# Attention on TensorE: 128-column products between 512-column ones, probabilities one unit later, the value product in one bank

## What is computed

```python
ada = (timestep_embed @ ada_w + ada_b)[:, None, :]
shift1, scale1, gate1, shift2, scale2, gate2 = jnp.split(ada, 6, axis=-1)
x1 = _ln(x) * (1.0 + scale1) + shift1
qkv = (x1 @ qkv_w + qkv_b).reshape(Bc, Tc, 3, H, DH)
q, k, v = (qkv[:, :, 0], qkv[:, :, 1], qkv[:, :, 2])
attn = jnp.einsum('bthd,bshd->bhts', q, k) * scale
attn = jax.nn.softmax(attn, axis=-1)
attn_out = jnp.einsum('bhts,bshd->bthd', attn, v).reshape(Bc, Tc, INNER)
attn_out = attn_out @ out_w + out_b
x = x + gate1 * attn_out
x2 = _ln(x) * (1.0 + scale2) + shift2
h = jax.nn.gelu(x2 @ ffn_w1 + ffn_b1, approximate=False)
x = x + gate2 * (h @ ffn_w2 + ffn_b2)
...
h = jnp.square(jax.nn.relu(jnp.einsum('bsd,hd->bsh', x, w1)))
return jnp.einsum('bsh,dh->bsd', _rms_norm(h), w2)   # w1, w2 ternary
```

## Time and profile before

| | |
|---|---|
| median of 3 runs | 390.71 us (390.7 to 392.43) |
| span of the profiled execution | 391.2 us |
| PE busy | 367.8 us (94%), 2096 matmuls |
| DVE busy | 288.0 us (74%) |
| ACT busy | 237.0 us (61%) |
| POOL busy | 129.7 us (33%) |
| mean granted clock of PE | 0.980 of full speed |

### The profile page before, as it was taken

The page is one execution under the profiler, slowest core; times in us unless marked ns, Lnnn a source line. Parts: engine busy times, 40 slices in busy tenths (PEclk is TensorE's granted clock), DMA queues, the critical chain, the costliest instruction groups (busy, mean ns, idle before and its releaser), DMA issues. The chain is left out here.

```text
span 391.2 us, 6260 instructions
## 1 busy us (share of the span) xinstructions
PE 367.8 (94%) x2096; PEld 319.5 (82%) x2096; DVE 288.0 (74%) x486; ACT 237.0 (61%) x582; POOL 129.7 (33%) x111
## 2 busy tenths in 40 slices
PE   2899999999999999999999999999889899996975
PEld 2789888888888888888888898889778787885855
DVE  5775569768776976866887667689988638797793
ACT  1464576665666566656676566775687358573751
POOL 1522224321542232272323144335423300162451
PEclk9999999999999999999999999999999999998995
DMA  7913031000303100030200012010000000000002
GB/s 231 358 61 108 1 109 54 2 0 3 108 0 107 54 0 0 0 107 29 78 0 0 0 26 83 0 55 1 2 0 1 2 0 2 0 1 2 8 19 80
DMA packets 11778, 16.53 MB, mean 42 GB/s; under 512 B 672, under 2 KB 7920, under 8 KB 11760
## 3 DMA queue, kind: packets, MB, share of 16 engines
q1 hardware_dynamic: 11760, 16.30, 12.6%
HBM read 15.25 MB, written 1.05 MB: 42 GB/s over the span
## 5 line engine op out<-in xcount | busy, mean ns | idle before, releaser
L345 POOL TENSOR_TENSOR prob<-prob,rinv 128x512 f32<-128x512 f32 x32 | 33.4, 1043 | 152.4 <-DVE rinv L788 152.4
L980 PE MATMUL bank<-x_hi,wqk_hi 128*128 128x512 f32 x128 | 54.4, 425 | 0.0
L982 PE MATMUL bank<-x_hi,wqk_lo 128*128 128x512 f32 x128 | 51.3, 401 | 0.0
L981 PE MATMUL bank<-x_lo,wqk_hi 128*128 128x512 f32 x128 | 51.1, 399 | 0.0
L706 DVE TENSOR_TENSOR v_lo<-bank,v_hi 128x512 fp32r<-128x512 f32 x30 | 20.7, 691 | 39.2 <-ACT v_hi L427 39.2
L493 ACT ACTIVATE prob<-bank,nbias 128x128 f32<-128x128 f32 x128 | 45.1, 370 | 4.1 <-DVE nbias L782 4.1
L427 ACT ACTIVATE p_split<-bank 128x512 fp32r<-128x512 f32 x32 | 19.1, 598 | 35.4 <-PE bank L1014 35.4
L461 ACT ACTIVATE o_hi<-pv_pair,bias 128x512 fp32r<-128x512 f32 x31 | 21.3, 688 | 24.3 <-PE pv_pair L1029 24.3
L982 PE MATMUL bank<-k_hi,q_lo 128*128 128x128 f32 x128 | 35.4, 276 | 0.0
L417 POOL TENSOR_TENSOR raw_qk<-raw_qk 128x512 f32<-128x512 f32 x13 | 18.4, 1415 | 50.7 <-ACT raw_qk L622 50.4
L981 PE MATMUL bank<-k_lo,q_hi 128*128 128x128 f32 x128 | 35.2, 275 | 0.0
(11 more groups left out here) (206 smaller groups left out, 1086.9 us busy)
## 6 DMA issues: line engine op xcount, KB each, us to landing
raw_qk<-in_L_cond_qkv_w_dram SPq DMA_DIRECT2D x8, 512.0 KB, 4.9
raw_v<-in_L_cond_qkv_w_dram SPq DMA_DIRECT2D x4, 512.0 KB, 3.8
raw_o<-in_L_cond_out_w_dram SPq DMA_DIRECT2D x4, 512.0 KB, 3.6
xt<-in_x_dram SPq DMA_DIRECT2D x2, 512.0 KB, 5.0
xr<-in_L_cond_ada_w_dram SPq DMA_DIRECT2D x1, 1024.0 KB, 10.2
raw_w<-in_L_cond_ffn_w_dram SPq DMA_DIRECT2D x2, 512.0 KB, 7.6
t_raw<-in_L_ffn_W_fc_dram SPq DMA_DIRECT2D x4, 256.0 KB, 3.8
t_raw<-in_L_ffn_W_proj_dram SPq DMA_DIRECT2D x4, 256.0 KB, 3.9
```

The lines of the kernel that those rows point to most:

```text
L345: nc.gpsimd.tensor_tensor(e, e, rinv[:, j % 2, :].unsqueeze(2).broadcast_to([P, SQ, P]), ALU.mult).then_inc(norm_done, 1)
L980: nc.tensor.matmul(dst, ah, bh, start=start and n == 0, stop=False)
L981: nc.tensor.matmul(dst, ah, bl, start=False, stop=False)
L982: m = nc.tensor.matmul(dst, al, bh, start=False, stop=stop and n == len(terms) - 1)
```

## The change

- On PE a unit starts with the 12 matmuls of q and k of unit i+1. Behind each of the first four stands one transpose, now of the probabilities of unit i-2, and behind the other eight one score matmul of unit i. A v block follows, one in each of the units 2 to 29, with the last four score matmuls and the first three of the value product; then the out product of unit i-3 with the other nine.
- The probabilities of unit i are transposed in unit i+2 and no longer in i+1, their value product is taken there as well, and the out product in i+3.
- The scores have two banks in turn (3 and 5), q and k two buffers in turn; the second buffers are parts of w2_hi and w2_lo, so half of the second FFN weight is cast after attention.
- The value product is 12 matmuls of 128 columns into bank 4, three a sequence, and its output one pass on DVE.
- Behind the loop, unit 30 has an order of its own ("early") and unit 31 is written out.
- ACT, DVE and POOL programs follow, with weight casts moved by one or two units; on POOL normalise stands behind them.

Bank table, ACT's and DVE's units:

```diff
-BQ, BK, BV, BS, BO, BY = 0, 1, 2, 3, 4, 6
+BQ, BK, BV, BO, BY = 0, 1, 2, 4, 6
+BS = (3, 5)
...
+        heads_q = ((q_hi[:, :], q_lo[:, :]), (w2_hi[:, w2_fourth], w2_lo[:, w2_fourth]))
+        heads_k = ((k_hi[:, :], k_lo[:, :]), (w2_hi[:, w2_third], w2_lo[:, w2_third]))
         w1_chunks, wv_chunks, wo_chunks = (
...
-        pv_main, pv_rest = (pv_pair[:, :].rearrange("p (s x t) -> p s x t", s=SQ, x=2)[:, :, n, :] for n in range(2))
+
+        bank = [ctx.enter_context(nc.psum_tensor(f"bank{n}", [P, TQ], F32)) for n in range(8)]
 
 
         cond_in, arow_in, bias_in, ada1_in, ada2_in = (
...
 
-        V_AT = {1: (4, 5), 2: (6, 7), 5: (0, 1), 6: (2, 3)}
...
+            def unit(G, j, last=False):
+                i = UG * G + j
+                known = isinstance(i, int)
+                early = known and i == NU - 2
+                if early:
+                    o_hi_part(*earlier(G, j, 3))
+                if not known or i >= 2:
+                    p_hi_part(i - 2)
+                q_hi_part(*later(G, j))
+                if not early and (not known or i >= 3):
+                    o_hi_part(*earlier(G, j, 3))
+                k_hi_part(*later(G, j))
+                load_weights(G, j, last)
+                if has_v(i):
+                    v_hi_part(V_AT[j], v_count(i))
+                if j == 5 and not last:
+                    for k in range(KD):
+                        wv_hi_part(k, 16 * G + 32)
+                softmax_exp(i, j)
 
...
+            def o_lo_part(G, j):
+                hi, lo = head_output(UG * G + j)
+                biased_lo(lo, bank[BO], HG * G + VB + j % HG, hi, o_h, UG * G + j + 1, o_l)
+
...
+            def unit(G, j):
                 i = UG * G + j
...
-                    dve.wait_ge(xr_done, 1)
-                    stats_of(2, xr)
-                if last and j == UG - 1:
-                    normalise(2, xr)
+                known = isinstance(i, int)
+                early = known and i == NU - 2
+                if early:
+                    o_lo_part(*earlier(G, j, 3))
+                if not known or i >= 1:
+                    softmax_inverse(i - 1, (j - 1) % 2)
+                if not known or i >= 2:
+                    p_lo_part(i - 2)
+                q_lo_part(*later(G, j))
+                if not early and (not known or i >= 3):
+                    o_lo_part(*earlier(G, j, 3))
+                if early:
+                    accumulate(i - 3, G, 0, last=True)
+                    softmax_max(i, j)
+                    gate(0)
+                    k_lo_part(*later(G, j))
```

The matmuls' steps, PE's unit, and PE's and DVE's programs behind unit 30:

```diff
+            def score_step(j, n):
+
+                (qh, ql), (kh, kl), t = heads_q[j % 2], heads_k[j % 2], slice(n // 3 * P, (n // 3 + 1) * P)
+                m = three(bank[BS[j % 2]][:, t], n % 3, qh[:, t], ql[:, t], kh[:, t], kl[:, t], True, True)
+                if n == 11:
+                    m.then_inc(s_mm, 1)
...
+            def pv_step(j, n):
+
+                a, quad, s = j % HG, j // HG, n // 3
+                b, h, t = quad * SQ + s, slice(a * P, (a + 1) * P), slice(s * P, (s + 1) * P)
+                m = three(bank[BO][:, t], n % 3, v_hi[:, b, h], v_lo[:, b, h], p_split[:, s, 0, :], p_split[:, s, 1, :], True, True)
+                if n == 11:
+                    m.then_inc(pv_mm, 1)
...
-                    b, h = quad * SQ + s, slice(a * P, (a + 1) * P)
-                    at = 2 * s * P
-
-                    nc.tensor.matmul(pv_pair[:, at:at + 2 * P], v_hi[:, b, h], p_split[:, s, :, :].rearrange("p x t -> p (x t)"),
-                                     start=True, stop=False)
-                    m = nc.tensor.matmul(pv_pair[:, at:at + P], v_lo[:, b, h], p_split[:, s, 0, :], start=False, stop=True)
-                m.then_inc(pv_mm, 1)
...
+            def unit(G, j):
...
-                    transpose_x(2, bank[0:2])
+                (G1, j1), (G2, j2), (G3, j3) = later(G, j), earlier(G, j, 2), earlier(G, j, 3)
+                VG = G + 1 if j in (6, 7) else G
+                early = known and i == NU - 2
+                pe.wait_ge(wqk_l, HG * G1 + j1 % HG + 1)
+                pe.wait_ge(q_l, i + 1)
+                t = not known or i >= 2
+                if t:
+                    transpose_ready(i - 2, v_count(i - 1) if not known or i - 1 <= V_LAST else v_count(V_LAST))
+                for n in range(6):
+                    q_or_k_step(G1, j1, 0, n)
+                    if t and n < 4:
+                        transpose_step(j2, n)
+                    else:
+                        if n == (4 if t else 0):
+                            scores_ready(G, j)
+                        score_step(j, n - 4 if t else n)
+                if early:
+                    out_ready(G3, j3)
+                    for n in range(6):
+                        out_step(G3, j3, n)
+                        score_step(j, n + 2)
+                for n in range(6):
+                    q_or_k_step(G1, j1, 1, n)
+                    if not t:
+                        score_step(j, n + 6)
+                    elif early and n < 4:
+                        score_step(j, n + 8)
+                    elif not early:
+                        score_step(j, n + 2)
...
+                if early:
+                    pv(G2, j2)
+                    return
+                pe.wait_ge(wv_l, KD * VG + KD)
+                pe.wait_ge(p_l, i - 1)
+                for n in range(6):
+                    v_step(VG, V_AT[j], n)
+                    if n < 4:
+                        score_step(j, n + 8)
+                    else:
+                        if n == 4:
+                            pv_ready(G2, j2)
+                            pv_step(j2, 0)
+                            pv_step(j2, 1)
+                        else:
+                            pv_step(j2, 2)
+                if known and i == 2:
+                    for n in range(3, 12):
+                        pv_step(j2, n)
+                    return
+                out_ready(G3, j3)
+                for n in range(6):
+                    out_step(G3, j3, n)
+                    if n % 2 == 0:
+                        pv_step(j2, 3 + n // 2 * 3)
+                        pv_step(j2, 4 + n // 2 * 3)
+                    else:
+                        pv_step(j2, 5 + n // 2 * 3)
...
+            for j in range(3, UG - 1):
+                unit(NG - 1, j)
+            L = NG - 1
+            transpose_p(NU - 3)
+            scores_ready(L, UG - 1)
+            for n in range(12):
+                score_step(UG - 1, n)
+            pe.wait_ge(gated, 1)
+            out_ready(L, UG - 4)
+            for n in range(6):
+                out_step(L, UG - 4, n)
+                if n < SQ:
+                    transpose_y_step(0, n)
+            pv(L, UG - 3)
+            transpose_p(NU - 2)
+            transpose_xr(0, bank[0:2])
+            out_product(L, UG - 3)
+            pv(L, UG - 2)
+            transpose_p(NU - 1)
+            out_product(L, UG - 2)
+            pe.wait_ge(xrT_done, 1)
+            transpose_x(2, bank[0:2])
+            pv(L, UG - 1)
...
+
+            softmax_inverse(NU - 2, (NU - 2) % 2)
+            p_lo_part(NU - 3)
+            o_lo_part(NG - 1, UG - 4)
+            softmax_max(NU - 1, UG - 1)
+            add_residual(0)
+            dve.wait_ge(xr_done, 1)
+            stats_of(2, xr)
+            o_lo_part(NG - 1, UG - 3)
+            p_lo_part(NU - 2)
+            softmax_inverse(NU - 1, (NU - 1) % 2)
+            normalise(2, xr)
             o_lo_part(NG - 1, UG - 2)
-            modulate(2, SHIFT2, SCALE2, bank[0:2], lambda: p_lo_part(NU - 1))
-            o_lo_part(NG - 1, UG - 1, h2[:, 0, :])
+            p_lo_part(NU - 1)
+            modulate(2, SHIFT2, SCALE2, bank[0:2])
+            o_lo_part(NG - 1, UG - 1)
             ternary_compare(NG - 1, -1)
```

453 lines of the change are left out of this document (209 added, 244 removed).

## The result

The changed kernel takes 413.36 us in the median of 4 runs (412.94 to 413.58), the kernel before 390.7 (390.65 to 392.43): a ratio of 1.0557, 95% interval 1.0524 to 1.0590. Slower, as forecast, by 22.7 us where I had said 15.0; 413.36 lies 1.4 us above the range.

What follows compares the result with a forecast made beforehand. PE was taken as the bound, attention being a stream without idle time. Profiled span 391.2 + 12.8 value product + 0 interleaving - 1.0 + 0.3 head + 2.9 tail = 406.2, less 0.5: 405.7 us, range 399 to 412.

Steps and rivals of the forecast that it cites:

- the fall: Head: granted clock drops to 0.50 around 38 to 40 us; nine 512-column matmuls there cost about 1.7 us more.
- One load ahead is all that happens: PE stream: in 512, 128, 512 columns the narrow matmul's load is hidden, the following wide one's is not.
- The value product: Attention units: four pairs (0.92 us) become 12 matmuls of 128 columns (1.32): +0.40 us a unit, +12.8 in 32.
- The sum of pitches doesn't depend on the order: Attention on PE: alternating narrow and wide matmuls costs the same total as grouping them, so 0 us.
- No new wait in the loop: Attention loop: PE gets no new wait; a unit takes 8.6 us and bank 2's chain has 0.9 us spare.
- The 7.9 for bank 2: Attention unit: bank 2's chain of transposes, value block and copies ends by 7.9 us; next transposes are due at 8.8.
- Tail: From unit 30's start to the first FFN matmul: waits of 6.7 us in place of 3.8, +2.9 (0 to +5).
- The median of the runs is 0.5 under that span: Last step of the sum: 0.5 us taken off the predicted span of 406.2 to give the median time.
- I expect the fall to be shorter or gone: -1.0: Head: wide matmuls directly behind the 8-column products shorten or remove the half-clock stretch, -1.0 us (0 to -1.7).
- +0.3: Head: units 1 and 2 have less work to cover k's hi and lo parts and hand-overs, +0.3 us.
- the interleaving term: Attention loop: some 24 narrow stretches a unit between wide matmuls, bounds +4 and -2 us, taken as 0.

Runs made afterwards that it cites:

- in blocks: The changed kernel with the same matmuls, but in each section of a unit first the wide ones, then the narrow ones: 416.39 us, ratio 1.0619.
- the one exchange: The changed kernel with the lo part of k for the last unit put ahead of the gating of y on VectorE in unit 30: 414.24 us, ratio 1.0572.

## Why the prediction missed

The direction, the mechanism in the loop and its price were right; the sum was 7.7 us short. Against an execution of the kernel before without the fall, head, loop, tail and FFN have 2.5, 13.7, 4.8 and 1.6 us more, where the prediction's terms give -0.3, 10.8, 4.5 and 0.

**Right.** *One load ahead is all that happens*: a pair is 0.34, with 128 columns or with 64. *The value product*: 1.34 in place of 0.92 us (+0.42, I said 0.40); alone in the old kernel it came to 402.8 where I had expected 403.5. *The sum of pitches doesn't depend on the order*: 8.67 us interleaved and 8.65 in blocks, though both a little above the old order (below). *No new wait in the loop*: none, but with less to spare than I had said. The 7.9 for bank 2 leaves out the 0.69 of the maximum that the same sentence names; with it the chain ends at 8.5, and 0.3 us are left, not 0.9. Its 0.2 for a hand-over is about what the trace of the kernel before has from PE to ACT: the last matmul of a value block starts at 75.42, the next one at 75.64, and ACT's copy at 75.84; from ACT to DVE it has less (0.03 for v, 0.14 to 0.16 for q and k).

**Right in part by luck.** *Tail*: 4.8 against 4.5. The new waits stand where I put them. But the trace of the kernel before has 2.5 us of waits in this stretch (1.04, 1.03, 0.22 and 0.20) and not 3.8, and the changed one 5.7 and not 6.7. The waits grew by 3.2 us, where I had said 2.9, and some 1.3 us that are neither listed waits nor in my count of matmuls stand in both kernels and cancel. That the waits come from VectorE's order was argued; the one exchange tried in it does not decide it.

**The failed step, first: the head.** *The median of the runs is 0.5 under that span*, and *I expect the fall to be shorter or gone: -1.0*. The two count the same fall twice. An execution's time is about 1.8 us over its span (390.3 and 388.5 in a later execution of the kernel before), and the median came out under the profiled span only because the profiled execution was one of the upper level: from the first 8-column product to the scores of unit 2 it takes 1.6 us longer with the fall (29.14 to 45.23) than without it (28.18 to 42.69). The three of the four first executions that lie at 390.65 to 390.71 are of the lower level, so the median has no fall to lose. The other term, *+0.3* for the k chain, was mis-sized and on the wrong chain: the changed head waits 1.60 us, 1.25 for the lo part of the probabilities and 0.35 for that of v, both in bank 2, whose chain I had priced for the loop only; for k it shows no wait. The head has 2.5 us more where my terms give -0.3, and some 0.5 of it is neither waits nor the value product and stays open.

The reason given for the -1.0, wide matmuls behind the 8-column ones, is not shown. Behind 32 of them wide ones went at half clock, so they don't prevent a fall (0.50 from 32 to 38 us). Yet the changed kernel keeps 16 in a row, with wide ones behind, and in the traces of it and of its ten traced variants the clock is 1.00 from 30 to 43 us. Why stays open.

**Second: the interleaving term, 0.** The loop has 13.7 us more, not 10.8. Of a unit's 0.50, the value product has 0.42 and the order 0.08. Interleaved, the wide matmuls behind a narrow one stand at 0.234, where I used 0.229 for all; in blocks they are 0.230 and 0.236, and the narrow ones 0.111 in place of 0.109. My own rows showed 0.24 for such a matmul and gave a bound of +4 us; I took 0, and into the range I put +2. With the +4 its upper end would be 413.3, just at the measured time. Why a wide matmul takes longer behind a narrow one is open.

**Third: a term that was missing, 1.6 us.** Behind the longer wait ahead of the FFN came a stretch at half clock (0.50 from 310 to 312), and with the wait filled it did not. I had put a price on waits, and none on what may follow them, although the trace of the kernel before had such a stretch in its ternary layer and I read its clock only in the head.

## What to carry to other kernels

Before pricing an order, find out from the starts of weight loads what a matmul costs at each width: here 128 columns cost as much as 64 or 8, and 256 hardly more (0.12), so a split of wide products into narrow ones is paid in full wherever they stand. Look at what the clock does behind each idle stretch of TensorE: it can cost a second time, though not every one does. Where the wait can't be shortened, fill it: dummy transposes gave 4 us here, and 2.5 in the kernel before. The deeper pipeline gained nothing in the loop and paid in head and tail (2.5 and 4.8 us), where units have less to cover their chains. A profiled execution is one draw: compare its span with the spread of times before taking a term off for something that only it may show.
